# Feature-pair network on one core: the fourth group's transposes placed four k-tiles later

## What is computed

```python
cont_emb = emb_table[:CONT_FIELD][None, :, :] * conts[:, :, None]
cate_emb = emb_table[cates]
cc = jnp.concatenate([cont_emb, cate_emb], axis=1)
gram = jnp.einsum('bfd,bgd->bfg', cc, cc)
pairs = gram[:, ROWS, COLS]
X = jnp.concatenate([cont_emb.reshape(cc.shape[0], -1), cate_emb.reshape(cc.shape[0], -1), pairs], axis=1)
X = jax.nn.relu(_layernorm(X @ W1 + b1, ln1_g, ln1_b))
X = jax.nn.relu(_layernorm(X @ W2 + b2, ln2_g, ln2_b))
logit = jax.nn.sigmoid(X @ Wout + bout)
```

## Time and profile before

| what | value |
|---|---|
| time, median of 3 runs | 777.32 us (774.78 to 778.52) |
| the profiled execution | 778.39 us, its span 776.9 us |
| TensorE (PE) busy | 731.6 us, 94% of the span |
| VectorE (DVE) busy | 582.2 us, 75% |
| ScalarE (ACT) busy | 516.1 us, 66% |
| GpSimd (POOL) busy | 481.3 us, 62% |
| granted TensorE clock, mean | 0.979 of full |

### The profile page before, as it was taken

How to read it: one execution, slowest core, us unless ns; L and a number is a source line. 1 busy time by engine, 2 the same in 40 slices (tenths; PEclk the granted TensorE clock), 3 DMA queues, 4 the chain that set the end, 5 groups by cost and what they waited for, 6 DMA issues and landing times.

```text
span 776.9 us, 11960 instructions
## 1 busy us (share of the span) xinstructions
PE 731.6 (94%) x3583; PEld 596.8 (77%) x3583; DVE 582.2 (75%) x1735; ACT 516.1 (66%) x978; POOL 481.3 (62%) x450
## 2 busy tenths in 40 slices
PE   5598899999999999999999999999999999999995
PEld 1356778888888888778788877878878888888884
DVE  7357977878878888787787877878787566565568
ACT  3487877868778687686867868677665535545441
POOL 6777877777777777777777777777000433434431
PEclk9798979999999999999999999999999999999998
DMA  8961111111111111111111111112463111101000
GB/s 323 347 228 25 23 54 28 54 54 26 54 39 40 52 25 52 34 45 52 25 54 25 52 54 26 52 25 59 176 216 124 55 29 54 54 27 54 27 1 0
DMA packets 26644, 53.37 MB, mean 69 GB/s; under 512 B 11024, under 2 KB 11351, under 8 KB 26554
## 3 DMA queue, kind: packets, MB, share of 16 engines
q1 hardware_dynamic: 10570, 31.29, 12.0%
q0 software_dynamic: 13312, 13.06, 7.3%
q10 hardware_dynamic: 2736, 8.71, 2.8%
HBM read 45.20 MB, written 11.63 MB: 73 GB/s over the span
## 4 chain that ended last, share of the span: by engine, by line
PE 44%; POOL 30%; issue 17%; DVE 4%; DMA 2%; ACT 2%; POOLq 0%; ACTq 0%; DVEq 0%
POOL xb L513 27%; PE acc L546 13%; PE acc L548 13%; PE acc L547 13%; POOL xb L510 3%; PE gr L612 1%; PE tr L612 1%; DMA xb<-in_L_rec_emb_table,idx_all 1%; PE gr L714 1%; PE tr L714 1%; DMA xb<-table_scratch,idx_all 1%; PE tr L570 0%; PE gr L570 0%; DMA last_row<-in_L_rec_emb_table 0%; ACT dots L830 0%
## 5 line engine op out<-in xcount | busy, mean ns | idle before, releaser
L513 POOL DMA_INDIRECT xb<-table_scratch,idx_all x390 | 381.3, 978 | 118.9 <-issue 116.4
L546 PE MATMUL acc<-w_hi,x_hl 128*128 128x512 f32 x416 | 172.9, 416 | 4.5 <-DVE x_hl L1115 3.1
L548 PE MATMUL acc<-w_hi,x_hl 128*128 128x512 f32 x416 | 165.5, 398 | 0.0
L547 PE MATMUL acc<-w_lo,x_hl 128*128 128x512 f32 x416 | 165.0, 397 | 0.0
L530 POOL TENSOR_TENSOR raw_lo<-raw_lo,raw_hi 128x1024 f32<-128x1024 f32 x14 | 33.5, 2391 | 146.8 <-ACT raw_lo L998 146.8
L546 PE MATMUL acc<-w_hi 128*128 128x512 f32 x256 | 100.9, 394 | 0.0
L548 PE MATMUL acc<-w_hi,w_lo 128*128 128x512 f32 x256 | 99.7, 389 | 0.0
L547 PE MATMUL acc<-w_lo,w_hi 128*128 128x512 f32 x256 | 99.7, 389 | 0.0
L794 ACT CAST g_still<-x_hl 64x384 fp32r<-64x384 f32 (+1 forms) x128 | 97.9, 765 | 2.5
L546 PEld LDWEIGHTS acc<-w_hi,x_hl 128*128 128x128 f32 x416 | 80.0, 192 | 20.8 <-issue 4.1
L548 PEld LDWEIGHTS acc<-w_hi,x_hl 128*128 128x128 f32 x416 | 79.7, 192 | 18.5
(11 more groups left out here) (121 smaller groups left out, 1313.3 us busy)
## 6 DMA issues: line engine op xcount, KB each, us to landing
raw_lo<-in_L_rec_W SPq DMA_DIRECT2D x26, 512.0 KB, 5.4
h_scratch<-h_row ACTq DMA_DIRECT2D x16, 512.0 KB, 2.9
raw_hi<-h_scratch SPq DMA_DIRECT2D x16, 512.0 KB, 3.5
xb<-table_scratch,idx_all POOLq DMA_INDIRECT x390, 2.4
table_scratch<-in_L_rec_emb_table SPq DMA_DIRECT2D x4, 781.2 KB, 7.9
raw_hi<-in_L_rec_W SPq DMA_DIRECT2D x6, 512.0 KB, 5.7
raw_hi<-in_L_rec_b SPq DMA_DIRECT2D x1, 512.0 KB, 4.3
raw_hi<-in_L_rec_ln_g SPq DMA_DIRECT2D x1, 512.0 KB, 5.2
```

Of the source, the lines that this page charges most:

```text
L513: done = nc.gpsimd.indirect_dma_start(out=to, out_offset=None, in_=table, in_offset=at_row)
L546: nc.tensor.matmul(o, a, w, start=first, stop=False)
L547: nc.tensor.matmul(o, a, v, start=False, stop=False)
L548: return nc.tensor.matmul(o, b, w, start=False, stop=last)
```

## The change

"own 3" moves in `STEADY` from behind k-tile 14 to behind k-tile 18, and in `LAST` from behind 15 to behind 18. Between it and gram 0 stand k-tiles 5, 6 and 7. The k-tiles between the later steps are dealt out anew: between gram 3 and "next 0" one k-tile (11), behind "next 0" one (12); in `LAST` gram 0 and gram 1 as well as gram 2 and gram 3 stand together, and "factor" goes behind k-tile 12. On ScalarE all four move copies of group 2 go ahead of the split of group 3; on VectorE `cont_features` goes ahead of it. `FIRST` and `SECOND` stay.

```diff
-STEADY = (0, "own 1", 1, 2, 3, "factor prev", 4, "own 2", "late prev", 13, 14, "own 3", 15, 16, 17, 18, 5,
-          "gram 0", 6, "gram 1", 7, "gram 2", 8, "gram 3", 9, 10, "next 0", 11, 12)
+STEADY = (0, "own 1", 1, 2, 3, "factor prev", 4, "own 2", "late prev", 13, 14, 15, 16, 17, 18, "own 3", 5, 6, 7,
+          "gram 0", 8, "gram 1", 9, "gram 2", 10, "gram 3", 11, "next 0", 12)
...
-LAST = (0, "own 1", 1, 2, 3, "factor prev", 4, "own 2", "late prev", 13, 14, 15, "own 3", 16, 17, 18, 5,
-        "gram 0", 6, "gram 1", 7, "gram 2", 8, "gram 3", 9, 10, 11, "factor", 12)
+LAST = (0, "own 1", 1, 2, 3, "factor prev", 4, "own 2", "late prev", 13, 14, 15, 16, 17, 18, "own 3", 5, 6, 7,
+        "gram 0", "gram 1", 8, "gram 2", "gram 3", 9, 10, 11, 12, "factor")
...
                 tail_features_hi(x - 1)
-                move_copies(x, 2, (0, 1))
+                move_copies(x, 2)
                 split_group(x, 3)
-                move_copies(x, 2, (2, 3))
                 gram_copies(x, 3)
...
                 tail_features_lo(x - 1)
+                cont_features(x)
                 split_group(x, 3)
                 still_low(x, 3)
-                cont_features(x)
```

## The result

The changed kernel took 800.27 us (median of 4 runs, 799.68 to 800.55) against 777.46 for the kernel before beside it; the ratio is 1.030, 95% interval 1.028 to 1.032. Its profiled execution took 800.55 us, the span 799.0, that is 22.1 us more than before.

The account below looks back on a forecast made before the run. POOL's gathers (33.3 us a tile against TensorE's 32.0) were taken to bound the kernel from tile 8. Passages 28.0, grams 1.4 and last tile 2.7, less stalls 8.5, gave + 23.6 us on 777.32: 801, range 793 to 809.

Parts of the forecast that it names:

- What bounds the kernel before: In the loop from tile 8: POOL's gathers, 33.3 us a tile against TensorE's 32.0, stall "own 3" by 8.5 us.
- (2) ScalarE between "own 3" and gram 0: Before gram 0: ScalarE is done 4.46 us after "own 3", TensorE ready at 4.45; gram 0 0 to 0.2 us late.
- the 0.1 that I counted for a weight load: At gram 0 of each tile: a start 0.1 us late, 1.4 us over 14 grams 0.
- (3) VectorE's chain: From gram 3 to k-tile 4: TensorE late by 0.4, 0.85 and 0.67 us at three steps, 2.05 us lost.
- the restart that I added to the 2.05: At k-tile 4, the last wait after gram 3: 0.1 us more, making 2.15 us a passage.
- (4) The last tile: Last tile: gram 3 waits 2.4 us, k-tile 13 comes about 14.9 us after gram 0; 2.74 us lost.
- the third rival: The clock falls once, in the last tile: 4 to 5 us more, 805 us; chance 0.15.
- The sum: Whole kernel: 28.0 (passages) + 1.4 (grams 0) + 2.7 (last tile) less 8.5 (stalls), net + 23.6 us.
- gather pace as the bound of both: Loop: POOL's gathers stay the bound and hide TensorE's new waits, 775.9 us; chance 0.10.
- w: Added time per loop tile over TensorE's 32.00 us: forecast 2.25 us, bounds 1.9 to 2.7.
- TensorE alone: Whole loop: the stalls come off and nothing takes their place, 768.8 us; chance 0.02.
- The clock falling in every tile: Loop: the clock falls for 10 us in each tile, 38 us on top, 839 us; chance 0.06.

## Why the prediction was right, point by point

**What bounds the kernel before**: right, and now shown. Relieving POOL gave 10.4 us by the medians and 8.0 by the spans (predicted 8.5), and 31.97 us a tile (32.00). That a late "own 3" brings at most 1.4 us as long as POOL sets the pace was argued from its fixed landing time; the run for it gave no verdict.

**(2) ScalarE between "own 3" and gram 0**: 4.50 us (4.45 + 0.1). The run with one k-tile there shows the same 4.49 without cover, so this distance is ScalarE's. What was wrong here is that the grams keep their spacing of 6.83 us: gram 0 to gram 3 takes 6.94 in every tile of the loop after, and gram 0 is shown 1.14 us long where it was 1.03. Its first weight load starts 0.01 us ahead of it after (234.60) and 0.23 ahead before (226.53). So the 0.1 that I counted for a weight load that no longer runs ahead is there, but in the gram, and beside the 0.06 in front of it.

**(3) VectorE's chain**: relative to gram 3, "next 0", k-tile 0 and k-tile 4 were predicted at 2.77, 5.46 and 12.31 us and came at 2.83, 5.44 and 12.34 in tile 4. That is the tile in which the prediction fits best; over tiles 2 to 14 they come at 2.82, 5.40 and 12.23 on average. The period was predicted at 34.25 and is 34.24 in this tile; over the loop, gram 0 of tiles 2 and 14 in the kernel after:

```profile
132.18 1.13 PE L612 MATMUL gr<-g_move,g_still 128*128 128x124 f32 x8
...
541.97 1.14 PE L612 MATMUL gr<-g_move,g_still 128*128 128x124 f32 x8
```

(541.97 - 132.18) / 12 = 34.15. The passage from gram 3 to k-tile 4 was counted at 10.26 + 2.15 = 12.41 us and takes 12.23, so the restart that I added to the 2.05 was one too many. Of these 0.18 the longer gram 0 takes a part back. Gram 0 of tile 2 to gram 0 of tile 15 is 575.95 - 132.18 = 443.77 us after and 555.24 - 130.85 = 424.39 before, 19.4 more, where the terms gave 13 x 2.25 less the stalls, 20.8: 1.4 us too much.

**(4) The last tile**: the 2.74 us ahead of gram 0 are there (2.8). The wait at gram 3 was put at 2.4 us and is 2.30; k-tile 13 was put at 14.9 us behind gram 0 and came 592.30 - 575.95 = 16.35 behind it. The forecast let VectorE's features set this; they were ready in time:

```profile
588.35 0.92 DVE L1167 TENSOR_TENSOR feats<-cc_rows,c 128x52 f32<-128x52 f32 x7
```

They end at 589.27, 13.3 us behind gram 0, but "factor" starts at 590.65: TensorE is what came late. From gram 3 to "factor" it takes 8.10 us, about 1.7 more than one gram and four k-tiles at full clock (0.95 + 4 x 1.37). So the 1.4 us are the clock's fall, the third rival, which happened beside the forecast. No run keeps the clock up there, so this rests on the timeline and on the same time in each of the three traces with the new LAST. The rival was right in kind and mis-sized: its 4 to 5 us were taken from a 10 us stretch at half clock in a slow start, but here, with k-tiles back to back behind the idle, the clock was full again from 587 us, 4 us after the idle's end.

**The sum**: + 23.6 predicted, + 22.1 in the profile. The terms account for the difference: - 1.4 (loop), + 1.4 (last tile), and - 1.5 from a place that the change does not touch: TensorE reached "next 0" of tile 2 at 109.30 before and at 107.81 after,

```profile
109.30 0.92 PE L570 MATMUL tr<-ident,xb 128*128 128x128 f32 x4
```

```profile
107.81 0.99 PE L570 MATMUL tr<-ident,xb 128*128 128x128 f32 x4
```

(the kernel before, then after), since the fall of the clock in tile 1 was shorter in that execution. It is chance: of the seven traces beside a before at 777, whose orders do not differ in tile 1, four reach that step at 109.3 to 110.2 us and three at 107.0 to 107.8. 23.6 - 1.4 + 1.4 - 1.5 = 22.1. So 801 came within 1 us of 800.3 by some luck: two small errors cancel, and a coincidence makes the rest. What stands by itself is the loop: 13 x (34.14 - 32.00) = 27.8 us measured, 29.3 predicted.

**The rivals**: gather pace as the bound of both would need w under 0.34; w is 2.14 over the loop. TensorE alone (768.8) is what the kernel before gives once POOL is relieved, not what this change gives. The clock falling in every tile did not come in this kernel, but it is what made two of the experiments 18 and 14 us slower than their chains say. The Trainium skill, "TensorE: Matmul & The Clock Gate", section "A second HAM failure mode: psum-queue depth-cycling", tells of a kernel in which frequent short idles made the clock oscillate. This trace doesn't agree for idles of 0.3 to 0.6 us, three a tile: the clock was 1.00 from 160 to 575 us.

## What to carry to other kernels

Work that is put between two steps of a tight order was taken from between two others: before judging the place that gains, walk the chain of the other engines beside the place that loses, from the step that starts it to the last one that waits for it. Waits that lie on one chain are not to be priced one by one; shortening an early one may lengthen the last. And look at what paces the stall that is to go: here a second engine, 1.2 us a tile slower than the first, capped the gain at 1.4 us (an estimate that no run with a verdict tested) before the cost was even counted.

## What the runs showed of the hardware that was not expected

**The clock after an idle of TensorE.** Idles of 0.3 to 1.1 us, once or three times a tile, left the granted clock at 1.00 over hundreds of us in the loop. Behind an idle of 2.3 to 2.6 us it fell to half in some tiles and not in others of the same kernel: with 2.60 us at gram 0, 8 of 12 tiles were 1.5 or 3.1 us longer than their chain; with 2.33 us at k-tile 4, 9 of 12 were 1.6 us longer; with 2.27 to 2.30 us at gram 3 of the last tile it fell in 3 of 3 traces, for 1.4 us each. Each fall thus cost 1.4 to 3.1 us on top of the idle. The idle alone does not decide it: in tile 1, where grams and single k-tiles alternate with waits, the clock also fell in all seven traces, in four of them behind an idle of 1.23 us, in three behind one of 1.2 and one of 1.95.

**The same kernel at 777 or at 955 us, by the chip.** In the experiments the kernel before took 777 to 778 us on two chips of five and 952 to 960 on three, each within 1.3% of its median. In the slow traces several engines stand still in the same stretch of each tile (VectorE up to 10.1 us, POOL 8.8 and the weight loads 9.7 in the run with "own 3" one k-tile later). From 300 to 305 us of that run, VectorE and ScalarE are not busy at all, TensorE for 0.99 us and POOL for 2.14, while single instructions last as long as before; TensorE's small matmuls start 0.7, 1.4 or 2.1 us apart there with "issue" as the mark. No run tests a cause: it is open.
